# An adaptive-norm transformer kernel: start loads on two queues, block 0's key products on DVE, the last modulations on DVE, and instruction lists placed anew

## The chip, the cores and the metric

The kernel runs on one core of one Trainium2 chip. The metric is device time in microseconds (us), the median of three runs. Engines are called as in the profile: PE (matrix engine), DVE (vector), ACT (scalar activations), POOL (GpSimd), and SP, which here only issues DMAs. ACT can issue DMAs too.

## What is computed

Two layers over x of 8 batches, 256 tokens and 128 features, all float32. Each layer normalises, scales and shifts the tokens with per-batch values (the modulation) made from a conditioning vector.

```python
# layer 0
h  = layernorm(x)*(1+ca) + sa                 # per batch
q,k,v = silu(conv4(silu(h @ W.T)));  q,k l2-normalised;  a,b = sigmoid(h @ Wa.T), sigmoid(h @ Wb.T)
for t in range(256):                          # per batch and head (16 heads of 8)
    S = a*S - a*b*outer(S@k, k) + b*outer(v, k);   o[t] = q @ S
x = x + ga*(o @ Wo.T + bo)
h2 = modulate(layernorm(x));  x = x + gb*(h2 + moe(h2))   # router, 8 experts 128->512->128, the two highest
# layer 1
x = x + ga1*(ssd(modulate(layernorm(x))) @ Wout.T)        # decaying sums along the tokens
x = x + gb1*ffn(modulate(layernorm(x)))                   # butterfly-parametrised 128->512->128, gelu
```

The gates are kept away from zero before use (a sign times at least 0.25), and the 18 butterfly stages of the last feed-forward are folded into two weight matrices on PE while the kernel runs.

## The kernel before

Features (or 16 heads times 8) lie on the 128 partitions, tokens in the free dimension. The 256 tokens are cut into five **windows** of 32, 32, 64, 64 and 64 tokens (`TWS`), each for all 8 batches; a **block** is 32 tokens (8 blocks: 0, 1, then two for each of windows 2 to 4), a **chunk** is 4 tokens (8 to a block). The recurrence over tokens is solved chunk by chunk on DVE: `chunk_seed` (L2254), `chunk_delta` (L2259), `chunk_outer` (L2273) and `chunk_scan` (L2282), four instructions for each of 64 chunks. They need two things that DMAs replicate over the partitions for a whole block, the normalised keys (`spread_keys`, L600, 8 DMAs into `krep`) and the solved keys (`spread_solved`, L614, 8 DMAs, and one at L616, into `wrep`). The solved keys come from a small triangular solve on DVE for each window: products of key pairs (`key_pairs`, L3275, on POOL) are summed over heads on PE (`key_products`, L758), `couple` (L2218) multiplies them by decays, and three pairs of `solve_product` (L2233) and `solve_rest` (L2242) update `XX`, whose first value POOL's `value` and `signed_key` (L3255, L3285) make.

Before that, each window passes layer norm (`center` L690 and `variance` L702 on PE, `ln_square` and `ln_scale` L1470 to L1482 on ACT, `ln` L2140 on DVE), `modulate` (L2155 and L2157 on DVE for the first two windows and the first experts' input, which are the list `WIDE`, else L1495 on ACT, one instruction per batch), five projections on PE (`project`), their activations on ACT (`projected`, L1521), a convolution of four taps (`first_tap` L1553 on ACT, `tap` L2206 on DVE), l2 norms (`square_sums` on PE, `norms` and `inverse_norms` L1577 to L1589 on ACT), and on POOL `key` (L3238), `query` (L3246), `scaled_key` (L3263), and the recurrence's helpers `decays` (L3296) and `read_state` (L3309). Behind a window's recurrence come the output projection (`attn_out`), the router, and the experts: `first` (L859) and `second` (L874) on PE with `hidden` (L1649) on ACT and `mix` (L2296) on DVE. Units 4 and 5 are the two halves of the batches of the last window; the last ssd and feed-forward are done in two halves too (numbered 3 and 4).

Nothing is scheduled by a compiler. Each engine has a hand-written list of calls (PE's begins at L943, ACT's at L1712, DVE's at L2543, POOL's at L3362, SP's at L627), it works through it in order, and every dependence is a semaphore wait inside the helper. So a waiting call holds up all calls behind it in its own list. A DMA is issued at its place in the list of the engine that issues it: SP's `loads` (L562), then the copies; ACT issues the first constant matrix (`load_center`) and the experts' weights (`load_weights`, L1460 and L1461, 2 MB each). `fold_up(i)` and `fold_down(i)` on PE (L782 to L801) with `folded` on ACT (L1595, L1597) fold the butterflies; `fold_load` on SP (L590) brings later stages' matrices into a ring of 8. `fill` (L941) is a matmul whose result nobody reads.

```python
            def key_pairs(n, g):          # POOL
                pool.wait_ge(s_kb_done, n + 1)
            def solve_product(n, j):      # DVE
                if j == 0:
                    dve.wait_ge(s_xk_init, n + 1)
            def chunk_seed(w, i):         # DVE, first chunk that reads wrep
                    dve.wait_ge(s_wrep_in[h % 2], 16 * DH * (h // 2 + 1))
```

## Time and profile before

| | |
|---|---|
| median of 3 runs | 488.26 us (487.59 to 488.83) |
| the profiled execution's own time | 488.68 us |
| its span in the profile | 486.1 us |
| PE, DVE, ACT, POOL busy | 426.6, 343.3, 363.9, 165.6 us |
| mean granted TensorE clock | 0.979 |
| last scan of the recurrence starts | 323.7 us |
| last output DMA lands | 486.1 us |

The span runs from the first to the last event in the trace; 2.6 us of the profiled execution's time lie outside it. All places below are us from the span's start. A row of a timeline merges neighbouring instructions of one line: start, length of the group, engine, line, what it writes and reads, count, and in brackets how long the engine idled before it and what ended that. A busy engine in a row of windows is counted with its small pipeline gaps closed.

### The profile page before, as it was taken

Reading aid. Unit: us, or ns where it says so; the run is one execution under the profiler, and the core shown is the slowest. Engines: PE = TensorE matmul, PEld = TensorE weight load, DVE = VectorE, ACT = ScalarE, POOL = GpSimd, SP = SyncE. Lnnn points to the kernel's source line nnn. Section 1 sums busy time; section 2 is a strip of 40 time slices with the busy share of each in tenths; the row PEclk is TensorE's granted clock in tenths of the full one; section 3 lists DMA queues with packets and bytes.
Section 4 is the critical chain, followed back from the end, with each engine's and each line's share of the span. In section 5 each row is a group of like instructions: output and inputs, shape, how many; then the busy total and the mean of one; then the engine's idle time right before and its main releaser. Section 6 shows DMA issues by size and latency. Waiting matters only on the chain. (4 is left out here: it accounts for less than half of the span.)

```text
span 486.1 us, 7168 instructions
## 1 busy us (share of the span) xinstructions
PE 426.6 (88%) x2168; PEld 312.2 (64%) x2168; DVE 343.3 (71%) x876; ACT 363.9 (75%) x643; POOL 165.6 (34%) x236
## 2 busy tenths in 40 slices
PE   3498797869998699999999999999999878999666
PEld 2395674547776576757676656776676646798434
DVE  1545988877899984999999899998434681212751
ACT  4849688876985669889669794849988888646544
POOL 1060860684165963365940173161200001000010
PEclk9859999889999999999999999999999999999999
DMA  7999635012830228300204801000001000000000
GB/s 194 315 365 252 221 87 122 2 50 66 224 79 0 55 50 216 99 0 13 76 1 114 213 6 23 1 1 0 2 0 24 0 1 1 23 1 1 0 0 22
DMA packets 34484, 35.46 MB, mean 73 GB/s; under 512 B 12808, under 2 KB 30608, under 8 KB 34192
## 3 DMA queue, kind: packets, MB, share of 16 engines
q1 hardware_dynamic: 34016, 30.77, 23.9%
q10 hardware_dynamic: 432, 4.26, 2.3%
q8 instruction: 17, 0.28, 0.2%
q14 instruction: 19, 0.16, 0.1%
HBM read 13.78 MB, written 1.05 MB: 31 GB/s over the span
## 5 line engine op out<-in xcount | busy, mean ns | idle before, releaser
L874 PEld LDWEIGHTS psS<-we2s,hid 128*128 128x128 f32 x1024 | 130.5, 193 | 33.2 <-issue 29.5
L859 PE MATMUL psF<-h,we1s 128*128 128x256 f32 (+1 forms) x384 | 135.7, 461 | 9.0 <-ACT hid L1649 8.3
L874 PE MATMUL psS<-we2s,hid 128*128 128x128 f32 x1024 | 131.8, 277 | 5.5 <-DVE acc L2296 5.5
L1649 ACT ACTIVATE hid<-psF,col 128x256 f32<-128x256 f32 (+1 forms) x192 | 99.2, 542 | 48.4 <-PE psF L859 42.9
L859 PEld LDWEIGHTS psF<-h,we1s 128*128 128x128 f32 x384 | 65.6, 192 | 43.9 <-issue 21.6
L3309 POOL TENSOR_TENSOR QS<-H,qn 128x256 f32<-128x256 f32 x64 | 52.5, 834 | 96.8 <-DVE H L2282 74.7
L2296 DVE SCALAR_TENSOR_TENSOR acc<-psS,gate,acc 128x128 f32<-128x128 f32 x128 | 40.6, 342 | 44.4 <-PE psS L874 44.0
L2282 DVE TENSOR_TENSOR_SCAN H<-A,psT 128x320 f32<-128x320 f32 x64 | 52.1, 814 | 1.2
L2254 DVE TENSOR_TENSOR psT<-wrep,H 128x360 f32<-128x360 f32 x63 | 42.9, 681 | 10.4 <-DMA wrep<-XX 8.6
L1449 ACT ACT_TABLE_LOAD x37 | 47.5, 1283 | 1.8 <-PEq L3614 1.2
L3360 POOL TENSOR_TENSOR x<-x,gdb 128x512 f32<-128x512 f32 (+1 forms) x5 | 4.4, 870 | 130.0 <-PE psM L690 129.0
L1447 ACT ACT_TABLE_LOAD x29 | 37.2, 1283 | 0.8 <-issue 0.3
L3296 POOL COPY A<-ag 128x256 f32<-128x256 f32 x64 | 30.4, 493 | 13.9 <-DVE H L2282 13.9
L2206 DVE SCALAR_TENSOR_TENSOR zb<-p,col,zb 128x512 f32<-128x512 f32 (+1 forms) x45 | 27.3, 646 | 7.2 <-ACT zb L1553 7.1
L2259 DVE TENSOR_REDUCE psT<-psT 128x32 f32<-128x288 f32 x63 | 29.1, 462 | 1.5
L815 PE MATMUL psB<-QS,worep 128*128 128x256 f32 x128 | 29.1, 381 | 0.0
L2273 DVE TENSOR_TENSOR psT<-krep,psT 128x256 f32<-128x256 f32 x63 | 26.8, 426 | 1.9
L690 PE MATMUL psM<-x,C 128*128 128x512 f32 (+3 forms) x36 | 17.8, 578 | 11.2 <-DMA x<-xT_dram 7.3
L815 PEld LDWEIGHTS psB<-QS,worep 128*128 128x128 f32 x128 | 24.1, 190 | 5.0 <-issue 1.7
L702 PE MATMUL psB<-sq,C 128*128 128x512 f32 (+3 forms) x36 | 18.0, 585 | 1.8 <-ACT sq L1470 1.8
L1495 ACT ACTIVATE hS<-hS,mod 128x64 f32<-128x64 f32 x48 | 16.5, 432 | 0.6 <-DVE hS L2140 0.6
L2539 DVE SCALAR_TENSOR_TENSOR x<-psM,mod,x 128x64 f32<-128x64 f32 x28 | 5.7, 276 | 15.7 <-PE psM L934 15.7
(264 smaller groups left out, 656.3 us busy)
## 6 DMA issues: line engine op xcount, KB each, us to landing
wrep<-XX SPq DMA_DIRECT2D x72, 160.0 KB, 3.4
krep<-kn SPq DMA_DIRECT2D x64, 128.0 KB, 2.5
hid<-fold_mats_dram SPq DMA_DIRECT2D x22, 256.0 KB, 4.4
we1s<-we_dram ACTq DMA_DIRECT2D x1, 2048.0 KB, 7.9
we2s<-we_dram ACTq DMA_DIRECT2D x1, 2048.0 KB, 13.7
outT_dram<-x SPq DMA_DIRECT2D x3, 256.0 KB, 2.6
M<-mats_dram SPq DMA_DIRECT2D x1, 576.0 KB, 4.3
x<-xT_dram SPq DMA_DIRECT2D x2, 256.0 KB, 7.1
```

Of the source, the lines that this page charges most:

```text
L815: last = mm(psB[:, at:at + HC], worep[:, e, :], QS[:, e, :], start=(e == 0), stop=(e == DH - 1))
L859: mm(bank[name][:, 0:(b - a) * TWS[w]], we1s[:, e, k * P:(k + 1) * P], h2[w % 2][:, a * TWS[w]:b * TWS[w]], start=True, stop=True).then_in ...
L874: last = mm(bank[name][:, t * P:(t + 1) * P], hid[n % 2][:, k, t * P:(t + 1) * P], we2s[:, e, k, :], start=(k == 0), stop=(k == HT - 1))
L1447: nc.scalar.preload_act_table_set(LN_EXP)
L1449: nc.scalar.preload_act_table(kind)
L1649: nc.scalar.activation(hid[x_ % 2][:, k, 0:c], psF[n % 2][:, 0:c], ACT.Silu, bias=pc("be1", HT * e + k)).then_inc(s_hid_done, 1)
L2254: v_.tensor_tensor(T9[:, :, :, :], wv, prev.unsqueeze(3).broadcast_to([P, DH + 1, NB, C9]), ALU.mult).then_inc(s_prod_done, 1)
L2259: v_.tensor_reduce(U[:, :, :], T9[:, :, :, 1:].rearrange("p e b i -> p b i e"), AX.X, ALU.add).then_inc(s_u_delta, 1)
L2282: v_.tensor_tensor_scan(H[g % NH_][:, 0:DH, :, :].rearrange("p e b i -> p (e b i)"), A9[g % NA][:, :, :, :].rearrange("p e b i -> p (e b i)"),
L2296: v_.scalar_tensor_tensor(acc[w % 2][:, at, :], psS[n % 2][:, t * P:(t + 1) * P], gate[w % 2][:, at, e:e + 1], acc[w % 2][:, at, :], ALU.m ...
L3296: g_.tensor_copy(A9[g % NA][:, :, :, 1:], a).then_inc(s_a9_done, 1)
L3309: g_.tensor_tensor(o, H[g % NH_][:, 0:DH, :, 1:], q, ALU.mult).then_inc(s_qs_done, 1)
```

## The change

1. **Loads on two queues.** ACT, behind `load_center`, now issues the first three projection matrices (`M[:, 0:3]`); SP issues the other six behind the second window's x, and with them the rest of the modulation weights, which were ahead of it.
2. **Key products of window 0 on DVE.** `key(0)`, `scaled_key(0)`, `key_pairs(0, 0)` and `key_pairs(0, 1)` leave POOL's list and stand in DVE's (new helpers there). Windows 1 to 4 keep them on POOL.
3. **Last modulations on DVE.** `modulate` of ssd 3, ssd 4, ffn 3 and ffn 4 leaves ACT for DVE, as one `tensor_scalar` with two per-partition scalars for each batch (4 to a call). The modulation of window 1's layer norm no longer waits for the second modulation's values, which it does not read.
4. **Four of block 0's eight solved-key copies** are issued by ACT (`SPLIT = 4`, new `spread_solved` there), the other four and the ninth by SP.
5. **Lists placed anew** on all engines. In the start, PE's second modulation and `fold_up(0)` stand ahead of `square_sums(0, .)`, a `fill` ahead of them, `load_weights` stands behind `folded(12)` instead of behind the gates; in the middle `mix`, `first`, `second`, router and recurrence calls change places by a few positions; in the end `fill`s move.

```diff
@@ sync @@
+                    if n == 1:
+                        sp.dma_start(M[:, 3:, :], mats[:, 3:, :]).then_inc(s_rest_in, 16)
+                        sp.dma_start(wm[:, 0, 2 * P:], wmod[:, 0, 2 * P:]).then_inc(s_fold_in, 16)
+                        sp.dma_start(wm[:, 1, :], wmod[:, 1, :]).then_inc(s_fold_in, 16)
                     if n == 0:
...
-                        sp.dma_start(M[:, :, :], mats).then_inc(s_mat_in, 16)
-                        sp.dma_start(wm[:, 0, 2 * P:], wmod[:, 0, 2 * P:]).then_inc(s_fold_in, 16)
-                        sp.dma_start(wm[:, 1, :], wmod[:, 1, :]).then_inc(s_fold_in, 16)
...
-                for e in range(DH):
+                for e in range(0 if h else SPLIT, DH):
@@ tensor, project @@
+                if n == 0 and i == 3:
+                    pe.wait_ge(s_rest_in, 16)
@@ scalar @@
                 nc.scalar.dma_start(C[:, 0, :], consts[:, 0, :]).then_inc(s_center_in, 16)
+                nc.scalar.dma_start(M[:, 0:3, :], mats[:, 0:3, :]).then_inc(s_mat_in, 16)
...
+            def spread_solved():
+
+                act.wait_ge(s_x_sub, CH - 1)
+                for e in range(SPLIT):
+                    nc.scalar.dma_start(wrep[0][:, e, :], XX[e::DH, 1, 0:HC // CH, :].rearrange("p g i -> p (g i)").unsqueeze(1).broadcast_to(
+                        [HEADS, DH, H9])).then_inc(s_wrep_in[0], 16)
@@ scalar, list @@
+            folded(3)
+            spread_solved()
+            projected(1, 3)
@@ vector, modulate @@
+                if key not in WIDE:
+                    for i, b in enumerate(ln_batches(key)):
+                        last = v_.tensor_scalar(out[:, i, :], out[:, i, :], mod[:, 6 * l + c, b:b + 1], mod[:, 6 * l + s, b:b + 1],
+                                                ALU.mult, ALU.add)
+                    last.then_inc(s_ln_h, 1)
+                    return
@@ vector @@
+            def key_pairs(n, g):
...
+                dve.wait_ge(s_kb_done, n + 1)
+                dve.wait_ge(s_qn_done, n + 1)
...
+                    v_.tensor_tensor(KK[:, g, at:at + bc * i].rearrange("p (g i) -> p g i", i=i), b3[:, :, j + 1:],
+                                     k3[:, :, j:j + 1].broadcast_to([P, bc, i]), ALU.mult).then_inc(s_kk_done, 1)
@@ sync, list @@
             spread_keys(1)
             spread_solved(1)
+            spread_keys(3)
             spread_keys(2)
             spread_solved(2)
             spread_solved(3)
-            spread_keys(3)
             spread_keys(4)
```

POOL in window 0, before, from the first value of `XX` to its last update (`kn`, `bg` and `zb` are the keys, the scaled keys and the pair products):

```order
L3296 COPY A<-ag 128x64x4
L3255 TENSOR_TENSOR XX<-zb,bg 128x64x4
L3238 TENSOR_TENSOR kn<-zb,norm 128x256
L3263 TENSOR_TENSOR bg<-kn,bg 128x256
L3246 TENSOR_TENSOR qn<-zb,norm 128x256
L3275 TENSOR_TENSOR zb<-bg,kn 128x192
L3275 TENSOR_TENSOR zb<-bg,kn 128x64
L3296 COPY A<-ag 128x64x4
L3275 TENSOR_TENSOR zb<-bg,kn 128x128
L3296 COPY A<-ag 128x64x4 x2
L3285 TENSOR_TENSOR XX<-bg,XX 128x64x4
```

The same stretch of POOL with the change:

```order
L3273 TENSOR_TENSOR XX<-G,na 128x64x4
L3298 TENSOR_TENSOR XX<-zb,bg 128x64x4
L3289 TENSOR_TENSOR qn<-zb,norm 128x256
L3339 COPY A<-ag 128x64x4 x6
L3328 TENSOR_TENSOR XX<-bg,XX 128x64x4
L3352 TENSOR_TENSOR QS<-H,qn 128x64x4 x2
```

`kn`, `bg` and the three products of POOL's list are gone from it, and all six `A` copies now stand ahead of the `XX<-bg,XX` that the solve waits for. DVE with the change, from `kn` to the solve's first steps:

```order
L2211 TENSOR_TENSOR kn<-zb,norm 128x256
L2219 TENSOR_TENSOR bg<-kn,bg 128x256
L2231 TENSOR_TENSOR zb<-bg,kn 128x192
L2231 TENSOR_TENSOR zb<-bg,kn 128x64
L2231 TENSOR_TENSOR zb<-bg,kn 128x128
L2254 TENSOR_TENSOR G<-psS,G 128x64x3
L2254 TENSOR_TENSOR G<-psS,G 128x64
L2254 TENSOR_TENSOR G<-psS,G 128x64x2
L2269 TENSOR_TENSOR norm<-G,XX 128x2x192
L2242 SCALAR_TENSOR_TENSOR zb<-p,col,zb 128x256
L2278 TENSOR_TENSOR XX<-XX,norm 128x2x64x3
L2269 TENSOR_TENSOR norm<-G,XX 128x2x128
```

These five key steps are new there; `zb<-p,col` (a tap of window 1) stands inside the solve.

ACT with the change, from `folded(0)` to its DMAs of the solved keys:

```order
L1603 ACTIVATE ssdb<-psM 128x516
L1450 ACT_TABLE_LOAD
L1527 ACTIVATE p<-psS,col 128x8x32 x2
L1601 ACTIVATE wc<-psF 128x512
L1527 ACTIVATE p<-psF,col 128x8x32
L1603 ACTIVATE ssdb<-psM 128x516
L1559 ACTIVATE zb<-p,col 128x256
L1479 ACTIVATE sq<-psM 128x512
L1559 ACTIVATE zb<-p,col 128x256 x2
L1448 ACT_TABLE_LOAD
L1489 ACTIVATE sq<-psB,eps 128x512
L1491 ACTIVATE sq<-sq 128x512
L1601 ACTIVATE wc<-psF 128x512
L1469 DMA wrep<-XX 128x1x320 x4
```

The four `wrep` copies stand behind window 1's first activations and the layer norm of window 2; before, ACT had no DMA here.

SP around block 2, before (a digit is the buffer, so `krep0` and `wrep0` are block 2's):

```order
L600 DMA krep1<-kn 128x1x256 x8
L614 DMA wrep1<-XX 128x1x320 x8
L616 DMA wrep1<-XX 128x320
L600 DMA krep0<-kn 128x1x256 x8
L614 DMA wrep0<-XX 128x1x320 x8
L616 DMA wrep0<-XX 128x320
L614 DMA wrep1<-XX 128x1x320 x8
L616 DMA wrep1<-XX 128x320
L600 DMA krep1<-kn 128x1x256 x8
```

and with the change:

```order
L602 DMA krep1<-kn 128x1x256 x8
L616 DMA wrep1<-XX 128x1x320 x8
L618 DMA wrep1<-XX 128x320
L602 DMA krep1<-kn 128x1x256 x8
L602 DMA krep0<-kn 128x1x256 x8
L616 DMA wrep0<-XX 128x1x320 x8
L618 DMA wrep0<-XX 128x320
L616 DMA wrep1<-XX 128x1x320 x8
L618 DMA wrep1<-XX 128x320
```

Block 3's keys (`krep1`, which wait until block 1's last `chunk_outer` has read the buffer) are now ahead of block 2's keys and solved keys; the same swap is made for blocks 5 and 7.

## Rows read from the trace of the kernel before

**Rows 1.** The page's parts 1 and 2: busy us of each engine, granted clock by slice.

```profile
PE 426.6 (88%) x2168; PEld 312.2 (64%) x2168; DVE 343.3 (71%) x876; ACT 363.9 (75%) x643; POOL 165.6 (34%) x236
PEclk9859999889999999999999999999999999999999
```

**Rows 2.** Windows: start:end, length, then busy us (x instructions) of PE, PEld, DVE, ACT, POOL, clock, DMA share, GB/s.

```profile
60.00:200.00 140.00, 121.94 (x623) 91.36 (x623) 117.88 (x252) 109.90 (x209) 77.23 (x109) 0.98 0.36 91
200.00:350.00 150.00, 149.08 (x747) 101.98 (x746) 136.45 (x332) 118.95 (x183) 63.44 (x80) 1.00 0.15 37
444.00:486.00 42.00, 27.54 (x118) 18.37 (x116) 20.01 (x67) 21.90 (x53) 1.22 (x2) 1.00 0.03 7
```

**Rows 3.** Timeline of PE and ACT, the first window's start.

```profile
10.88 1.22 PE L690 MATMUL psM<-x,C 128*128 128x256 f32 x2 [2.65 <-DMA x<-xT_dram]
...
13.07 0.48 ACT L1521 ACTIVATE p<-psS,col 128x264 f32<-128x264 f32 x1 [3.16 <-issue]
```

**Rows 4.** Timeline of ACT, POOL and DVE, from the norms to the first step of solve 0.

```profile
27.00 0.63 ACT L1589 ACTIVATE norm<-norm 128x512 f32<-128x512 f32 x1
...
27.70 0.72 POOL L3238 TENSOR_TENSOR kn<-zb,norm 128x256 f32<-128x256 f32 x1 [0.78 <-ACT norm L1589]
...
32.97 0.70 POOL L3285 TENSOR_TENSOR XX<-bg,XX 128x256 f32<-128x256 f32 x1
...
34.59 0.69 DVE L2218 TENSOR_TENSOR G<-psS,G 128x192 f32<-128x192 f32 x3 [2.18 <-PE psS L758]
35.41 0.56 DVE L2233 TENSOR_TENSOR norm<-G,XX 128x384 f32<-128x384 f32 x1
```

**Rows 5.** Groups of ACT by form, 27.7 to 46: busy us, mean ns, idle before.

```profile
L1447 ACT ACT_TABLE_LOAD x1 | 1.3, 1283 | 0.0
L1597 ACT ACTIVATE ssdb<-psM 128x516 f32<-128x516 f32 x3 | 1.8, 590 | 2.9 <-PE psM L782 2.9
```

**Rows 6.** Timeline of DVE, one instruction's line alone and beside POOL.

```profile
9.11 0.43 DVE L2155 TENSOR_TENSOR hf<-hf,mod 128x264 f32<-128x264 f32 x1
...
31.13 0.63 DVE L2155 TENSOR_TENSOR hf<-hf,mod 128x256 f32<-128x256 f32 x1
```

**Rows 7.** SP's and DVE's timelines, the DMA view (KB each, us to landing), a window: solved keys of block 0.

```profile
28.45 7.60 SPq L600 DMA_DIRECT2D krep<-kn  x8
...
39.79 5.37 SPq L614 DMA_DIRECT2D wrep<-XX  x8
...
48.91 0.54 DVE L2254 TENSOR_TENSOR psT<-wrep,H 128x360 f32<-128x360 f32 x1 [4.45 <-DMA wrep<-XX]
...
wrep<-XX SPq DMA_DIRECT2D x72, 160.0 KB, 3.4
...
45.00:50.00 5.00, 4.63 (x35) 3.96 (x34) 1.02 (x3) 4.52 (x10) 1.30 (x4) 1.00 0.92 243
```

**Rows 8.** The DMA view and DVE's timeline: the experts' second weights, block 2's first seed.

```profile
we2s<-we_dram ACTq DMA_DIRECT2D x1, 2048.0 KB, 13.7
...
81.38 0.54 DVE L2254 TENSOR_TENSOR psT<-wrep,H 128x360 f32<-128x360 f32 x1 [0.20 <-issue]
```

**Rows 9.** Timelines of DVE and SP, block 1's last outer product to block 2's copies.

```profile
107.38 0.42 DVE L2273 TENSOR_TENSOR psT<-krep,psT 128x256 f32<-128x256 f32 x1
...
105.11 5.08 SPq L600 DMA_DIRECT2D krep<-kn  x8
118.57 5.34 SPq L614 DMA_DIRECT2D wrep<-XX  x8
```

**Rows 10.** Timelines of ACT, PE and DVE in the end.

```profile
471.64 1.42 ACT L1495 ACTIVATE krep<-krep,mod 128x64 f32<-128x64 f32 x4
...
473.88 1.28 ACT L1449 ACT_TABLE_LOAD   x1
...
478.35 1.89 PE L934 MATMUL psM<-krep,wc 128*128 128x256 f32 x8
...
449.15 0.86 DVE L2397 SCALAR_TENSOR_TENSOR x<-psS,mod,x 128x64 f32<-128x64 f32 x4 [0.53 <-PE psS L885]
```

More of the change, by code:

```diff
@@ L1325, in _ @@
                 first(4, 4, i)
-            fill(39)
+            second(4, 3, 0)
             first(4, 4, 3)
-            first(4, 5, 0)
-            second(4, 3, 0)
             second(4, 3, 1)
-            for i in range(1, 4):
+            for i in range(0, 4):
                 first(4, 5, i)
+            first(4, 6, 0)
             second(4, 4, 0)
             second(4, 4, 1)
-            first(4, 6, 0)
             ssd_out(2)
@@ L1380, in _ @@
             first(5, 4, 1)
-            center(("ssd", 3))
             second(5, 3, 0)
@@ L1789, in _ @@
             modulate(("front", 3))
-            for i in range(0, 3):
-                hidden(0, 3, i)
+            hidden(0, 3, 0)
+            hidden(0, 3, 1)
             projected(3, 0)
+            hidden(0, 3, 2)
             hidden(0, 3, 3)
@@ L2013, in _ @@
                 hidden(4, 3, i)
-            for i in range(0, 3):
-                hidden(4, 4, i)
+            hidden(4, 4, 0)
+            hidden(4, 4, 1)
+            ssd_factors(2)
             ssd_gate(2)
@@ L2055, in _ @@
             ln_scale(("ssd", 3))
-            modulate(("ssd", 3))
             ssd_steps(3)
@@ L2060, in _ @@
             ssd_in(3)
-            modulate(("ssd", 4))
             ssd_steps(4)
@@ L3485, in _ @@
-            for i in range(4, 8):
+            decays(3, 11)
+            for i in range(3, 6):
+                read_state(3, i)
+            decays(3, 12)
+            conv_taps()
+            read_state(3, 6)
+            decays(3, 13)
+            read_state(3, 7)
+            decays(3, 14)
+            value(4)
+            key(4)
+            read_state(3, 8)
+            attn_gate(4)
+            experts_gate(2)
+            read_state(3, 9)
+            decays(3, 15)
+            scaled_key(4)
```

1201 lines of the change are left out of this document (599 added, 602 removed).

## The prediction

> **What bounds the kernel now.** I read the page's busy line first: PE is the busiest engine and its granted clock is at the upper level (2.4 GHz) in nearly every slice, low only in single early ones [rows 1]. The windows then say where a change can pay. From 200 to 350 us PE is busy 149.08 of 150 us: there only less PE work, or work that comes earlier, shortens anything. From 60 to 200 it is busy 121.94 of 140, and in the last 42 us only 27.54, with DVE at 20.01 and ACT at 21.90 [rows 2]. In those last us no engine is full, so each step of the chain counts at its own length. The third view is the timeline ahead of the first seed of the recurrence: a chain of single instructions from the first activation through norms, keys and solve to DMAs. The recurrence, and with it most of what PE does later, hangs on it.
>
> **The loads.** The first `center` begins at 10.88, after 2.65 us of idle that a DMA of x ends; the first activation at 13.07 follows 3.16 us of ACT's idle [rows 3]. In the change x's second part no longer stands behind six projection matrices and most of the modulation weights, and `M[:, 0:3]` has SP's place to itself. The gain is at most the idle of 3.16 us, and it can be nothing if the bytes ahead of x were not what made it late; a loss here would need M's first part to come later than x, and it is the first thing on ACT's queue after one small constant. I take half, 1.5 us. The norms then end at 27.63 [rows 4] less 1.5, 26.1.
>
> **Key products on DVE.** Before: norms end 27.63, POOL's `kn` at 27.70 takes .72, and the last thing that the solve waits for, `XX<-bg,XX`, ends at 32.97 + .70; `couple` comes at 34.59 behind 2.18 us of waiting for PE, the solve at 35.41 [rows 4]. After: two 128x256 products at .63 each and 384 elements of pair products, some 1.05 us, end at 28.4 (.63 is the price of such an instruction beside POOL, .43 alone [rows 6]; by .43 it is 27.7). PE's key products then need banks that ACT's first activations of window 1 free. ACT passes one fold (.59), a table load (1.28) [rows 5] and two activations of .48 [rows 3], 2.8 us, so to 28.9, and `couple` (.69 [rows 4]) is done by about 30.2. POOL meanwhile has one product of .73, six copies of about .43 and the signed key at .70 (the prices of the products are from [rows 4], that of the copies is taken between .40 and .46), 6.0 less the first value of `XX` that it starts early, so about 30.3. All three meet at 30.4, where the solve starts, 5.0 us earlier, the loads' 1.5 included.
>
> Here a row speaks against the change: the same instruction on DVE took .43 us with POOL quiet and .63 with POOL at work [rows 6]. By these prices the moved work loses 46% to contention and is still shorter than POOL's chain. The Trainium skill ("SBUF — State Buffer", section "SBUF: two separate sides") calls this pair of ports an exclusive lock, held for a whole instruction of DVE with two SBUF inputs against one of POOL, and not a shared rate. By that rule POOL's nine instructions and DVE's five would alternate: 6.0 + 2.3 from 26.1, so the solve at 34.4, only 1.0 earlier.
>
> It needs no page to be a rival: the .20 of rows 6 could be a whole instruction's wait (.4 to .7) where both engines have denser work.
>
> **The solve** ran from 35.41 to SP's next issue at 39.79 [rows 4, 7], 4.35 us, with two taps of window 1 in it. In the change one of them (about .48) stands behind the solve, and the copies of constants too: 3.4 us, end 33.8, 6.0 earlier.
>
> **Spread of the solved keys.** SP's eight key copies took 7.60 us from 28.45 [rows 7]; they begin with `kn`'s end and, 1 to 2 us earlier, stay ahead of the solve's end as before. Nine issues of some .65 then end at 45.8, the first seed follows at 48.91 after 4.45 us of waiting for these DMAs, one copy taking 3.4 us to land; from 45 to 50 the DMA engines are busy to .92 at 243 GB/s [rows 7]. The split removes four issues from SP, 4 × .67 = 2.7 us by issue time. Against it: ACT reaches its four only behind some 13 activations of about .56 and two table loads of 1.28 [rows 3, 5], 9.8 us, with 1 us of waits for PE, so at 36.9, and issues till 39.6. Plus 3.4 that is 43.0. SP's five begin at 34.3 and end at 37.6. So the first seed comes at about 42.8, 6.1 earlier, and the split itself is worth nearly nothing. Were it free of ACT's list, it would be 40.8. The Trainium skill ("DMA: Bandwidth & Descriptors", section "Issuing engines are not separate DMA queues") has it that issuing on several engines saves only the issue time, all transfers running on the same 16 engines. With the share of .92 of rows 7 even the 2.7 us would be doubtful.
>
> ACT's own cost: 2.7 us of issue in front of `projected(1, 3)`, hidden as long as window 1 isn't the end of the chain (its first seed is some 20 us away); with the cover gone it is 2.7 us.
>
> **The middle.** The experts' second weights took 13.7 us to land [rows 8]. Issued behind `folded(12)`, at about 52, they are there by 66, and the first experts run at about 75: no cost, and the copies of block 0 no longer share the DMA engines with them. Window 1's chain is 5.5 to 6 us earlier too, since its inputs are, and block 2's first seed (81.38 [rows 8]) moves to about 75.5. From 200 us on PE has no idle in which an earlier arrival could be lost [rows 2], so the head's gain reaches the tail whole. I put the moves of `mix`, `router` and the rest at 0, between −3 (18 us of PE idle between 60 and 200 is there to be found [rows 2]) and +6 (the whole of the head's gain lost in it).
>
> **The tail.** `modulate` of ffn 3 took 1.42 us on ACT [rows 10], and four such instructions on DVE took .86 with a PSUM input [rows 10], so at most that: −.56. The table load at 473.88 stood behind ACT's work and now begins about .45 earlier, and the next modulation no longer splits ACT's gelu calls: the down projection that ran from 478.35 to 480.24 [rows 10] starts some 1.8 us earlier. I take −1.8 for the feed-forward, between −.5 (only the shorter modulation) and −3 (both modulations of 1.42 gone from ACT and the chain). In the ssd the same move gains .6 for half 4, but `ln` and `modulate` of half 3 now stand ahead of the residual that follows `experts` at 449.15 [rows 10] and delay it by .5 to .75: 0. Behind the waiting modulations DVE holds residuals that are not ready sooner, so the wait costs nobody.
>
> **The sum.** Head −6.1, middle 0, tail −1.8: −7.9 from the profiled execution's 488.68 gives 480.8. That execution is .42 above the median of the runs, so I forecast **480.5 us**.
>
> **Rivals.**
> - *The forecast's case*, 0.60: the head's shift passes through.
> - *Part of the head's gain is eaten*, 0.18: the port of rows 6 blocks for whole instructions (+4 by the working above), or ACT comes to its four copies 2 to 3 us late because of its two table loads and waits for PE. The seed then comes at 45 to 46. For it speaks that ACT's copies are the last of all steps in my sum; against it, that POOL's chain has been shortened by four instructions. Price 3 to 4 us: 484.
> - *The middle gains too*, 0.12: the moved calls fill some of PE's 18 idle us between 60 and 200, and the lower clock there goes. Some 3 us more: 477.5. Against: nothing in the rows shows that the places of these calls were what made PE wait.
> - *Slower than before*, 0.06: the order on SP. Before, SP issued block 2's keys from 105.11 for 5.08 us and its solved keys from 118.57 [rows 9]. Now block 3's keys stand ahead of both, and they wait for block 1's last outer product, which ended at 107.38 + .42 = 107.80 [rows 9]. Two sets of keys, 2 × 5.2, are 10.4 us of issue between 107.80 and 118.54, the end of the solve: room for 10.7. It just fits, if this distance is kept. But the last outer product comes earlier or later with the recurrence, the solve with PE's projections; each us by which the distance shrinks delays block 2's second set, hence all later chunks, by one. To lose more than the 7.9 gained and 1.5 besides, the distance must fall below about 1.3 us. At its worst the sum is 480.8 + 10.4 = 491. For: block 5's and 7's keys have the same swap. Against: the outer products move with the same head, so both ends shift together.
> - *The change doesn't do what it says*, 0.04: the second queue brings x no sooner (the bytes share the same engines) and the four copies wait behind ACT's list while the products on DVE wait for the banks that ACT frees. Then only the tail and part of the key chain are left: −3 to −4, 485.
>
> **Numbers.** The measurement can tell some 0.3%, 1.5 us, from no change. Forecast's case, eaten, middle and the failed second queue are all faster. A loss of up to 7 us in SP's order or the middle brings it to the same or near. Faster 0.87, the same 0.05, slower 0.08 (the 0.06 and other waits of the new lists). For the range: the forecast's own terms give −1.2 and +1.8 on the tail, ±1.5 on the loads, so 477.5 to 483.5; eaten and failed cases reach 485 to 486, the middle's case 476. Range 476 to 486; left out are the slower case, some of the eaten and the far end of the middle.
>
> **What would show it.** Right: first activation at about 11.5; solve starting at 30 to 31; the first seed near 43, waiting for the copies that ACT issued; block 2's first seed near 75.5; last scan of the recurrence near 318; first down projection 1.5 to 2 us nearer to the end; table load behind half 4's inverse root, with no L1495 between gelu calls. Wrong: the first activation still at 13 (loads), DVE's key products at .8 or more each (port), first seed beyond 45 (spread), a seed of block 2 or 3 waiting over 2 us for `wrep` (SP's order), a shift of the head of 6 us that is 3 at 200 us (middle), or experts' first matmul waiting for its weights.

## The result, and the profile after

The changed kernel takes **493.45 us** (median of 4 runs, 491.94 to 495.33); before, in the same comparison, 488.54. The ratio is 1.008, 95% interval 1.005 to 1.011: slower by 3.9 us (2.4 to 5.4). The forecast was 480.5 in a range of 476 to 486. All us of a difference below are a ratio times 489, with its interval.

The page's busy line and clock after, against [rows 1]. PE's busy time grew by 4.5 us and its mean clock fell from .979 to .969:

```profile
PE 431.1 (88%) x2164; PEld 313.1 (64%) x2164; DVE 351.3 (72%) x897; ACT 359.8 (73%) x627; POOL 166.9 (34%) x231
...
PEclk9878999979999899999999999999999999999899
```

The windows, with the columns of [rows 2]:

```profile
60.00:200.00 140.00, 120.11 (x594) 88.49 (x594) 114.55 (x244) 107.93 (x206) 74.81 (x100) 0.95 0.43 117
200.00:350.00 150.00, 147.31 (x739) 100.59 (x738) 140.07 (x333) 115.52 (x175) 65.68 (x84) 1.00 0.15 36
```

From 60 to 200 PE is busy 1.8 us less than before, at a granted clock of .95 instead of .98; from 200 to 350 again 1.8 us less: PE does less work in the same stretch. When the scans of the recurrence begin shows where the time went (us; in brackets the distance to before; block and chunk count from 0):

| scan of | before | changed | start and end only (r1) | middle only (r4) |
|---|---|---|---|---|
| block 0, chunk 1 | 50.59 | 48.69 (−1.9) | 48.39 (−2.2) | 50.28 (−.3) |
| block 2, chunk 0 | 129.20 | 127.94 (−1.3) | 127.54 (−1.7) | 128.84 (−.4) |
| block 3, chunk 6 | 169.92 | 170.57 (+.7) | 168.24 (−1.7) | 169.76 (−.2) |
| block 4, chunk 0 | 191.05 | 194.53 (+3.5) | 189.92 (−1.1) | 193.55 (+2.5) |
| block 6, chunk 0 | 272.09 | 280.92 (+8.8) | 270.84 (−1.3) | 280.54 (+8.5) |
| block 7, chunk 7 | 323.65 | 330.91 (+7.3) | 322.44 (−1.2) | 330.59 (+6.9) |

The changed kernel is still 1.0 us ahead when block 3 begins (151.36 for 152.39) and loses in two stretches, from there to block 4 and from block 4 to 6. From the last scan to the end of the span it takes 160.4 us where the kernel before took 162.5, so some 2 of the 7.3 us come back.

The start of the timeline, ACT and then PE, against [rows 3, 4]:

```profile
6.53 0.22 ACT L1459 ACTIVATE csil<-csil 128x16 f32<-128x16 f32 x1 [3.40 <-DMA col<-cols_dram]
...
11.21 0.39 ACT L1479 ACTIVATE sq<-psM 128x256 f32<-128x256 f32 x1 [1.84 <-PE psM L692]
11.61 1.28 ACT L1450 ACT_TABLE_LOAD   x1
12.90 0.85 ACT L1527 ACTIVATE p<-psS,col 128x264 f32<-128x264 f32 x2
...
25.81 0.84 ACT L1583 ACTIVATE norm<-psS,eps 128x256 f32<-128x256 f32 x2 [1.96 <-PE psS L751]
...
28.09 0.63 ACT L1595 ACTIVATE norm<-norm 128x512 f32<-128x512 f32 x1
...
9.98 1.19 PE L692 MATMUL psM<-x,C 128*128 128x256 f32 x2 [1.00 <-DVE hf L2143]
...
19.09 2.49 PE L720 MATMUL psM<-csil,wrep 128*128 128x8 f32 x20 [2.62 <-DVE hf L2143]
22.00 2.06 PE L786 MATMUL psM<-ssdb,hid 128*128 128x129 f32 x8 [0.42 <-DVE mod L2175]
23.86 1.91 PE L751 MATMUL psS<-norm,C 128*128 128x256 f32 x4
```

PE's `center` of window 1 no longer waits for x: it runs at 9.98 instead of 10.88. But ACT's first activation, which waits for the DMA of `col`, comes at 6.53 where it came at 5.61 (that DMA took 4.2 us to land, 3.3 before), and window 0's layer norm and modulation are 1.0 us later with it, done at 10.99. So the first projections begin at 11.14 instead of 11.89, .75 us earlier. ACT then squares window 1's layer norm at 11.21 ahead of its table load, and the first activation comes at 12.90 (13.07 before). Then PE's modulation and first fold (2.06 us from 22.00) stand in front of the square sums, and the norms' first activation waits 1.96 us for them. The last inverse norm ends at 28.72, 1.1 us later than before.

DVE's key products, the solve, the copies of the solved keys on SP and ACT, the first seed, and ACT's copies in the DMA view, against [rows 4, 7]:

```profile
28.83 0.98 DVE L2211 TENSOR_TENSOR kn<-zb,norm 128x256 f32<-128x256 f32 x1 [3.37 <-ACT norm L1595]
29.90 0.44 DVE L2219 TENSOR_TENSOR bg<-kn,bg 128x256 f32<-128x256 f32 x1
30.38 1.23 DVE L2231 TENSOR_TENSOR zb<-bg,kn 128x192 f32<-128x192 f32 x3
33.46 0.56 DVE L2269 TENSOR_TENSOR norm<-G,XX 128x384 f32<-128x384 f32 x1
...
37.79 3.36 SPq L616 DMA_DIRECT2D wrep<-XX  x4
...
39.72 2.25 ACTq L1469 DMA_DIRECT2D wrep<-XX  x3
...
47.15 0.54 DVE L2290 TENSOR_TENSOR psT<-wrep,H 128x360 f32<-128x360 f32 x1 [3.49 <-DMA wrep<-XX]
...
wrep<-XX ACTq DMA_DIRECT2D x4, 160.0 KB, 4.3
```

`kn` took .98 us, the other steps .44 and 1.23 for three. The solve starts at 33.46, 2.0 us earlier than before, and ends 2.2 earlier. SP issues four copies from 37.79 and ACT its last three from 39.72; the first seed stands at 47.15 instead of 48.91, after 3.49 us of waiting for these DMAs. From the first issue to the seed it is 9.4 us with two queues, 9.1 before with one, and ACT's copies took 4.3 us to land where SP's take 3.4.

PE's longest waits in the middle, and windows in which its clock was at the lower level (1.2 GHz) part of the time:

```profile
101.61 3.75 PE L878 MATMUL psS<-we2s,hid 128*128 128x128 f32 x16 [3.79 <-DVE acc L2332]
...
157.90 3.66 PE L751 MATMUL psM<-norm,C 128*128 128x512 f32 x4 [2.50 <-DVE x L2433]
...
168.07 3.01 PE L863 MATMUL psF<-h,we1s 128*128 128x256 f32 x6 [2.78 <-ACT hid L1655]
```

```profile
98.00:108.00 10.00, 6.39 (x24) 5.31 (x24) 6.57 (x14) 9.83 (x18) 6.92 (x7) 0.66 0.11 27
168.00:172.00 4.00, 3.93 (x14) 3.14 (x15) 3.90 (x8) 1.81 (x5) 3.92 (x5) 0.58 0.64 163
460.00:466.00 6.00, 4.54 (x12) 3.38 (x12) 5.71 (x18) 2.45 (x8) 0.00 (x0) 0.72 0.00 0
```

Before, past the start, PE's clock was at the lower level at 92 to 95 and 102 to 105 only. The changed kernel has a stretch of 7 us at 100 to 107 and others at 42 to 45, 157 to 161, 168 to 171 and 462 to 465, each at a wait of PE of 2.5 to 3.8 us.

SP's copies, and DVE's first seed and outer product for block 6. Changed:

```profile
246.73 5.84 SPq L602 DMA_DIRECT2D krep<-kn  x8
265.66 5.48 SPq L616 DMA_DIRECT2D wrep<-XX  x8
...
271.89 5.26 SPq L602 DMA_DIRECT2D krep<-kn  x8
...
273.77 1.63 DVE L2565 SCALAR_TENSOR_TENSOR x<-psM,mod,x 128x64 f32<-128x64 f32 x8 [1.22 <-PE psM L923]
275.32 0.53 DVE L2290 TENSOR_TENSOR psT<-wrep,H 128x360 f32<-128x360 f32 x1
...
280.46 0.43 DVE L2309 TENSOR_TENSOR psT<-krep,psT 128x256 f32<-128x256 f32 x1 [1.53 <-DMA krep<-kn]
```

and before:

```profile
228.98 5.04 SPq L600 DMA_DIRECT2D krep<-kn  x8
...
259.58 5.44 SPq L614 DMA_DIRECT2D wrep<-XX  x8
...
268.70 0.54 DVE L2254 TENSOR_TENSOR psT<-wrep,H 128x360 f32<-128x360 f32 x1 [1.28 <-DMA wrep<-XX]
...
271.44 0.42 DVE L2273 TENSOR_TENSOR psT<-krep,psT 128x256 f32<-128x256 f32 x1
```

Block 7's keys were issued at 246.73, and block 6's own keys only at 271.89, behind its solved keys; before, block 6's keys were issued at 228.98. So the first outer product of block 6 waited for `krep`, and it ran at 280.46 instead of 271.44. That wait is only part of these 9.0 us. The first seed of block 6, which reads no `krep`, is 6.6 us late already (275.32 for 268.70), and its solved keys are issued 6.1 us late. In front of it DVE now has an `ssd_residual` (L2565) that waited 1.22 us for PE and took 1.63; before, that call stood behind the seed. From the seed to the outer product it is 5.1 us instead of 2.7.

The end, against [rows 10]:

```profile
461.08 0.83 PE L904 MATMUL psS<-krep,M 128*128 128x256 f32 x2 [2.49 <-DVE krep L2159]
461.70 3.49 PE L915 MATMUL psB<-xi,taps 128*128 128x256 f32 x8
...
477.65 0.98 DVE L2159 TENSOR_SCALAR krep<-krep,mod 128x64 f32<-128x64 f32 x4
...
475.06 0.38 ACT L1479 ACTIVATE sq<-psM 128x256 f32<-128x256 f32 x1 [2.66 <-PE psM L692]
...
479.82 1.28 ACT L1450 ACT_TABLE_LOAD   x1
481.11 0.84 ACT L1715 ACTIVATE krep<-psM,ubias 128x256 f32<-128x256 f32 x2
...
483.53 1.89 PE L938 MATMUL psM<-krep,wc 128*128 128x256 f32 x8
```

The modulation takes .98 us on DVE for four (1.42 on ACT) and the table load is directly followed by the gelu calls. From ACT's square of the first feed-forward norm (475.06; 468.71 before) to the first down projection (483.53; 478.35 before [rows 10]) it is 8.5 us instead of 9.6. The eight matmuls of the first ssd convolution took 3.49 us at the lower clock; before they took 1.89.

### The profile page after: what moved, and what is told of

It is laid out like the page before. It is cut to its first block and busy times, and to the rows that moved or that the text cites. A ratio compares the mean times of both kernels' runs of the same rounds, so it can differ in the third digit from the quotient of the medians.

```text
span 491.3 us, 7161 instructions
## 1 busy us (share of the span) xinstructions
PE 431.1 (88%) x2164; PEld 313.1 (64%) x2164; DVE 351.3 (72%) x897; ACT 359.8 (73%) x627; POOL 166.9 (34%) x231
## 3 DMA queue, kind: packets, MB, share of 16 engines
HBM read 13.78 MB, written 1.05 MB: 30 GB/s over the span
## 5 line engine op out<-in xcount | busy, mean ns | idle before, releaser
L863 PE MATMUL psF<-h,we1s 128*128 128x256 f32 (+1 forms) x384 | 137.5, 464 | 8.9 <-ACT hid L1655 7.9
L878 PE MATMUL psS<-we2s,hid 128*128 128x128 f32 x1024 | 133.8, 278 | 8.5 <-DVE acc L2332 8.4
L1655 ACT ACTIVATE hid<-psF,col 128x256 f32<-128x256 f32 (+1 forms) x192 | 100.4, 543 | 54.1 <-PE psF L863 46.2
L3352 POOL TENSOR_TENSOR QS<-H,qn 128x256 f32<-128x256 f32 x64 | 55.0, 866 | 99.6 <-DVE H L2318 80.2
L3339 POOL COPY A<-ag 128x256 f32<-128x256 f32 x64 | 32.1, 525 | 0.0
```

Of the source, the lines that this page charges most:

```text
L863: mm(bank[name][:, 0:(b - a) * TWS[w]], we1s[:, e, k * P:(k + 1) * P], h2[w % 2][:, a * TWS[w]:b * TWS[w]], start=True, stop=True).then_in ...
L878: last = mm(bank[name][:, t * P:(t + 1) * P], hid[n % 2][:, k, t * P:(t + 1) * P], we2s[:, e, k, :], start=(k == 0), stop=(k == HT - 1))
L1655: nc.scalar.activation(hid[x_ % 2][:, k, 0:c], psF[n % 2][:, 0:c], ACT.Silu, bias=pc("be1", HT * e + k)).then_inc(s_hid_done, 1)
L3339: g_.tensor_copy(A9[g % NA][:, :, :, 1:], a).then_inc(s_a9_done, 1)
L3352: g_.tensor_tensor(o, H[g % NH_][:, 0:DH, :, 1:], q, ALU.mult).then_inc(s_qs_done, 1)
```

## The experiments

Sixteen kernels ran, each compared with the kernel before in the same set. "Middle" is all calls between about 60 us (PE behind `center(("front", 3))`, DVE from `chunk_seed(1, 0)`) and 444 us (PE from `second(5, 6, 0)`, DVE from `ln(("ssd", 3))`). A list put in another order holds the same calls, except that the changed order has no `fill(39)` in the middle.

How far single traces can be trusted shows in four kernels whose lists are those of before up to block 4, but for SP's in r6 (r3, r6, r8, r16): their scan of block 4 is −1.5, +.3, −.9 and −.1 us from that of before. So a distance to before of 1.5 us in one trace says little. From block 2 on such a distance changes by at most .6 us within one trace where the lists are the same.

| run | kernel | us, median | against before, us (interval) |
|---|---|---|---|
| | changed | 493.45 | +3.9 (2.4 to 5.4) |
| r1 | changed start and end | 487.70 | −1.6 (−2.8 to −.5) |
| r2 | changed start | 489.09 | −.1 (−1.0 to +.8) |
| r3 | changed end | 488.30 | −.6 (−1.9 to +.6) |
| r4 | changed middle | 494.84 | +5.0 (3.3 to 6.8) |
| r5 | changed, SP's order of before | 491.77 | +3.2 (2.2 to 4.3) |
| r6 | before, SP's changed order | 493.16 | +4.0 (2.6 to 5.4) |
| r7 | before, other lists 60 to 190 changed | 493.10 | +4.1 (2.6 to 5.5) |
| r8 | before, other lists 190 to 444 changed | 491.45 | +2.4 (1.5 to 3.3) |
| r9 | r1, start mended | 485.43 | −3.0 (−4.4 to −1.7) |
| r10 | r9 without the split | 485.53 | −3.2 (−4.4 to −2.1) |
| r11 | r7 with 2 unread matmuls | 490.79 | +2.1 (1.1 to 3.1) |
| r12 | r9 with 6 unread matmuls in the middle | 486.46 | −2.5 (−3.8 to −1.3) |
| r13 | r9 with 3 unread matmuls in the end | 485.64 | −3.3 (−4.5 to −2.1) |
| r14 | mended start, old end, modulations on DVE | 487.36 | −1.7 (−2.7 to −.6) |
| r15 | mended start only | 487.30 | −1.7 (−2.8 to −.5) |
| r16 | before, only block 7's keys moved on SP | 491.34 | +2.4 (1.5 to 3.3) |

### Which stretch (r1 to r4)

The theory was that the middle's order costs some 7 us; the rival, that the start's change harms the middle. r1 is the changed kernel with the middle's calls in the order of before:

```diff
             first(0, 0, 3)
-            logits(0)
             first(0, 1, 0)
-            second(0, 0, 0)
             first(0, 1, 1)
+            logits(0)
             first(0, 1, 2)
+            second(0, 0, 0)
...
```

> The changed kernel with its lists between about 60 and 444 us put back in the order of before; start (loads, key products, split copies, start of the lists) and end stay as changed. Theory O (the new order of the middle costs some 7 us, head gives about 1, tail about 2 to 3): about 485, 3 us under before. Rival P (the head's change itself harms the middle, by earlier but unevenly placed arrivals): 492 to 494, as the changed kernel.

Measured 1.6 us under before, at 487.7: the rival falls, and the theory's 485 was 2.7 too good. r2 takes the end back too (`modulate` of the four last norms on ACT again):

```diff
@@ vector @@
-            modulate(("ffn", 3))
@@ scalar @@
+            modulate(("ffn", 3))
...
```

> Only the start as changed, middle and end in the order of before, last modulations on ACT. Theory O: 487, 1 us under before, since the first seed of the recurrence came 1.8 us earlier in the changed kernel and PE is full from 200 us on. Rival P: 494 or more.

Measured −.1, and its profile's first chunk was 1.1 us later than before (51.66): the start is worth about nothing as it stands. The four traces with this start have the first seed at 47.15, 46.85, 50.12 and 48.56, the eight with the start of before between 48.43 and 49.62: on average .7 us earlier. r3 is before with the DVE helper and the end's lists of the change:

```diff
@@ vector @@
             ln(("ssd", 3))
+            modulate(("ssd", 3))
...
@@ tensor @@
-            fill(43)
...
```

> Only the end as changed: the four last modulations on DVE and the end's lists. Theory O and the tail's term of the prediction: 2 us under before, 486.5. Rival: the end as changed brings nothing because the stretch at the lower clock at 462 to 465 us of the changed kernel comes with it: 488 to 489.

Measured −.6 with an interval that holds both zero and the theory's −2. r4 is before with the changed order of the middle on all five engines:

```diff
             spread_solved(1)
+            spread_keys(3)
             spread_keys(2)
...
```

> The kernel before with nothing but the lists between about 60 and 444 us in the changed order. Theory O: 7 us slower than before, 495. Rival P: within 1.5 us of before.

Measured +5.0: the middle alone more than accounts for the loss, as theory O said; its size was 5 and not 7. The pieces that were changed outside the middle then take back 1 us.

### Which part of the middle (r5 to r8)

r5 and r6 undo and make SP's order alone:

```diff
-            spread_keys(3)
             spread_keys(2)
             spread_solved(2)
             spread_solved(3)
+            spread_keys(3)
...
-            spread_keys(7)
             spread_solved(6)
-            spread_keys(6)
...
```

> The changed kernel with nothing but SP's later copies put back in the order of before (block 2's keys and solved keys ahead of block 3's keys, and so for 5 and 7). Theory S (window 4's recurrence starts 8 us late because its first keys are issued behind block 7's keys and block 6's solved keys, and the end follows it): the first outer product of block 6 back to within 2 us of before, and the time at 487, 6 us under the changed kernel. Rival L (the lists of PE, DVE, ACT and POOL between 60 and 444 us cost the 5 us, PE being full while window 4 waits): 492 to 494, although block 6 starts earlier.

> The kernel before with nothing but SP's later copies in the changed order. Theory S: block 6's first outer product 8 us later than before and the time 5 us over before, 494. Rival L: block 6 late all the same, but the time within 1.5 us of before, since PE has experts' work to fill the wait.

r6 is 4.0 slower: SP's order does cost by itself, and PE's full stretch doesn't hide it. Its scans are within .7 us of before up to block 5 (191.31 for 191.05 at block 4) and 2.9 late at block 6. DVE waits there for `krep`, and PE then for the `mix` behind it on DVE:

```profile
274.36 0.43 DVE L2276 TENSOR_TENSOR psT<-krep,psT 128x256 f32<-128x256 f32 x1 [2.16 <-DMA krep<-kn]
...
283.50 1.73 PE L877 MATMUL psS<-we2s,hid 128*128 128x128 f32 x8 [2.26 <-DVE acc L2299]
```

But r5, where SP's order is put back in the changed kernel, is only .7 under the changed kernel, well inside the intervals, and its block 6 is still 7.3 us late (279.40). So theory S is right about a cost and wrong about it being the cause: in the changed kernel the other lists make block 6 late too, as its seed did above (275.42 in r5, 275.32 in the changed kernel). r7 and r8 take these lists alone, in two stretches:

```diff
@@ tensor, r7 @@
             attn_out(2)
-            square_sums(3, 0)
+            first(1, 3, 2)
             variance(("front", 4))
-            first(1, 3, 2)
+            square_sums(3, 0)
             square_sums(3, 1)
-            first(1, 3, 3)
             second(1, 2, 0)
             second(1, 2, 1)
+            first(1, 3, 3)
...
```

> The kernel before with PE's, ACT's, DVE's and POOL's lists between 60 and about 190 us in the changed order, SP as before. Theory S: within 1.5 us of before. Rival L: 2 to 4 us over before, since the changed kernel was 4 us behind at the first scan of window 3 (194.5 for 191.1).

> The kernel before with these lists between about 190 and 444 us in the changed order, SP as before. Theory S: within 1.5 us of before. Rival L: 1 to 3 us over before.

Rival L holds for both: +4.1 and +2.4. In r7 the distance to before is .7 at 170 us and 2.7 at the first scan of block 4, and stays at 3.2 to the last scan; window 3's solve begins at 177.22 and its solved keys are issued at 183.05, 180.09 before. In r8 it is −.9 at block 4, 4.1 at block 6 and 2.8 at the last scan. The three parts sum to 10.5 us and the whole middle costs 5.0. The traces show part of the overlap: from block 4 to block 6 r8 loses 5.0 and r6 2.7, but r4, which has both, 6.0; and from the last scan to the end r4 takes 161.6 us; r6, r7, r8 and before take 162.1 to 162.5. What the rest is was not followed.

### The clock (r11, r12)

r11 is r7 with two matmuls that nobody reads in PE's wait ahead of `second(1, 2, 0)`:

```diff
+            def fill_b():
+                free("B")
+                mm(psB[:, 0:4 * P], cst("ident"), C[:, :, :].rearrange("p a n -> p (a n)"), start=True, stop=True)
...
             square_sums(3, 1)
+            fill_b()
+            fill_b()
             second(1, 2, 0)
```

> The kernel of the seventh run (before, with the lists of 60 to 190 us in the changed order) plus two matmuls that nobody reads on the bank of the layer norm's variance, ahead of second(1, 2, 0), where PE idled 2.12 us and its granted clock then fell to 0.5 for 5 us. Theory C (the idle lets the clock fall, and this is most of the loss): no fall at 162 to 168, the shift of 3.2 us shrinks below 1, time 490 against the seventh run's 493.1. Rival W (the waits of the new order cost it, clock or no clock): 493.

The window 160 to 170 of r7, and then of r11:

```profile
160.00:170.00 10.00, 7.53 (x25) 5.54 (x26) 9.62 (x22) 7.39 (x10) 8.46 (x13) 0.66 0.10 24
```

```profile
160.00:170.00 10.00, 7.60 (x35) 5.37 (x34) 9.59 (x22) 7.93 (x11) 8.46 (x11) 0.86 0.23 57
```

The granted clock rose from .66 to .86; a lower stretch remains at 167 to 171. The runs put r11 at 2.1 us over before and r7 at 4.1, but the two intervals meet, and the profiles don't give the difference to the fill. r11's scans are 1.6 us ahead of r7's at the start of block 2 (128.06 for 129.68) and of block 3 (150.78 for 152.42), before anything differs in the lists; behind the fill they are 1.2 ahead at block 4 and 1.4 at the last scan. From block 3 to block 4 r7 loses 2.6 us and r11 3.0. So the higher clock gained nothing that these traces show, and rival W is left: the new order's waits cost the time, clock or no clock. r12 puts six into the mended kernel:

```diff
+            fill_b()
+            fill_b()
+            fill_b()
             second(0, 2, 0)
...
+            fill_b()
             square_sums(3, 1)
...
+            fill_b()
+            fill_b()
             second(1, 2, 0)
```

> The mended kernel of this set with six such unread matmuls: three ahead of second(0, 2, 0), where PE idled 3.74 us and the clock fell for 7 us, one ahead of square_sums(3, 1) and two ahead of second(1, 2, 0). Theory C: no lower clock between 98 and 108 and between 160 and 168, 5 us under the same kernel without them, 480. Rival W: the same time as without them, within 1 us.

The window 98 to 108 without them (r9) and with them (r12):

```profile
98.00:108.00 10.00, 7.87 (x30) 5.87 (x31) 6.83 (x16) 8.71 (x18) 9.06 (x11) 0.83 0.39 100
```

```profile
98.00:108.00 10.00, 7.06 (x32) 4.40 (x31) 6.86 (x16) 8.70 (x18) 9.37 (x13) 1.00 0.39 99
```

The clock is whole, and the time is the same within the intervals: 3.5 us ahead of before at block 4 instead of 3.4. So the lower clock there cost nothing that was on the chain, and theory C, with its 480, falls. The Trainium skill ("TensorE: Matmul & The Clock Gate", section "Part 1: The HAM clock gate") has PE fall to 1.2 GHz when it idles; the rows agree that a wait comes with each lower stretch named here (the shortest, .91 us, ahead of 447 in r9), and add that neither of the two filled here had a price that can be seen.

### The start (r9, r10, r15)

r9 is r1 with two calls moved:

```diff
@@ tensor @@
             modulation()
-            fold_up(0)
             square_sums(0, 0)
             square_sums(0, 1)
+            fold_up(0)
@@ scalar @@
-            ln_square(("front", 1))
             projected(0, 0)
             projected(0, 1)
+            ln_square(("front", 1))
```

> The first run's kernel (changed start and end, middle in the order of before) with two calls moved: PE's square sums of window 0 ahead of the first fold instead of behind it, and ACT's square of window 1's layer norm behind the first two activations, as before, instead of ahead of them and of their table load. Theory H (the new order of the start gave back what the loads and the key products gained): first activation at about 12.0 instead of 12.9, last inverse norm ended at 25.7 instead of 28.3 to 28.7, first seed at 44 instead of 47, time 3 us under the first run's 487.7, 484.7. Rival D (the spread of the solved keys over the DMA engines sets the first seed): norms 2.5 us earlier but the seed within 1 us of 47, time 487.

```profile
12.48 0.48 ACT L1547 ACTIVATE p<-psS,col 128x264 f32<-128x264 f32 x1 [1.77 <-issue]
...
23.89 0.84 ACT L1603 ACTIVATE norm<-psS,eps 128x256 f32<-128x256 f32 x2
...
26.18 0.63 ACT L1615 ACTIVATE norm<-norm 128x512 f32<-128x512 f32 x1
...
45.26 0.54 DVE L2354 TENSOR_TENSOR psT<-wrep,H 128x360 f32<-128x360 f32 x1 [4.12 <-DMA wrep<-XX]
```

The first activation comes at 12.48, the norms start at 23.89 without waiting, the last ends at 26.81 and the first seed is at 45.26, 3.7 us earlier than before, though later than the 44 of theory H. Rival D falls: against the changed kernel the norms' end and the seed both come 1.9 us earlier. The distance to before is 3.4 at block 2, 3.4 at block 6 and 3.4 at the last scan: what the start gains passes through the middle whole when the middle is in the order of before. How much it gains is less sure. Six traces have this start (r9, r10, r12 to r15), and they are ahead of before at block 4 by 3.4, 2.9, 3.5, 1.3, .8 and 3.0 us, 2.5 on average; the start alone, r15, is 1.7 faster in time. The time of r9 is 3.0 under before; it is the fastest of the kernels here, with r10, r12 and r13, which cannot be told from it.

r10 has SP issue all nine copies. The kernel that ran also had the two moved calls, which its expectation does not say, so it is to be read against r9:

```diff
-SPLIT = 4
+SPLIT = 0
...
             folded(3)
-            spread_solved()
             projected(1, 3)
```

> As the first run's kernel, with all nine copies of block 0's solved keys issued by SP and none by ACT. The prediction's term (the split is worth nearly nothing): first seed within 1 us of 46.5 to 47.2, time 487 to 488.5. Rival: issue time counts, and the seed comes 2.7 us later at 49.5, time 490.

First seed at 45.79 against 45.26, time within .2 us of r9: the split is worth nothing that can be measured. r15 leaves the end as it was:

```diff
@@ vector @@
-            modulate(("ssd", 3))
@@ scalar @@
+            modulate(("ssd", 3))
...
```

> The start as changed with the two calls moved, middle and end of before, modulations on ACT. The start's shift of 3.4 us passes through PE's full stretch whole: 485.5 to 486. Rival: the end as changed carried part of the ninth run's gain, and this is at 487.

487.3, 1.7 under before: the rival's figure, though its interval reaches to −2.8. So the end's change may carry 1.3 us of r9's 3.0, as between r2 and r1 (1.5); each of the two is inside the intervals. The profiles don't show this gain: from the last scan to the end the kernels with the changed end and the old middle take 161.7 to 163.1 us (r1, r3, r9, r10, r12, r13), before and r2 162.5 and r15 163.0.

### The end (r13, r14)

```diff
@@ r13, tensor @@
+            fill(61)
             ssd_steps(3)
...
+            fill(59)
+            fill(51)
             ssd_steps(4)
```

> The mended kernel of the ninth run with three more unread matmuls in the end: one ahead of ssd_steps(3) and two ahead of ssd_steps(4), where PE idled .91 and 2.49 us and its granted clock stood at 0.5 from 447 to 458. Theory C (the lower clock there costs the end part of its gain): no lower clock from 446 to 458, the 8 matmuls of the first ssd convolution take 1.9 instead of 3.6 us, and the time is 2 us under the ninth run's 485.4, 483.5. Rival: within 1 us of it, as the six fills of the middle were.

The first ssd convolution in r9, then in r13:

```profile
453.34 3.62 PE L918 MATMUL psB<-xi,taps 128*128 128x256 f32 x8
```

```profile
454.45 1.89 PE L918 MATMUL psB<-xi,taps 128*128 128x256 f32 x8
```

The eight matmuls take 1.89 us again, but the clock fell later (460 to 466) and the time is that of r9: no gain. r14 keeps the end's lists of before and puts each modulation on DVE behind its `ln`:

```diff
@@ vector @@
             ln(("ffn", 3))
+            modulate(("ffn", 3))
             ln(("ffn", 4))
+            modulate(("ffn", 4))
@@ scalar @@
-            modulate(("ffn", 3))
-            modulate(("ffn", 4))
```

> Mended start, middle and end in the order of before, the four last modulations on DVE directly behind their normalisation. If the modulations are the gain and the end's new order costs: 2 us under the run with the old end (r15), 484. If the new order of the end is part of the gain: 485 to 486.

The same as r15 (487.36 and 487.30), so neither the 484 nor the 485 to 486 came: the move of the modulations to DVE gives nothing without the end's new order.

### Which swap on SP (r16)

```diff
             spread_keys(5)
-            spread_keys(6)
+            spread_keys(7)
             spread_solved(6)
+            spread_keys(6)
             spread_solved(7)
-            spread_keys(7)
```

> The kernel before with only the keys of block 7 moved ahead of block 6's solved keys and keys on SP; the swaps of blocks 3 and 5 are not made. If the last swap is what costs on SP: the first scan of block 6 2.9 us late, 4 us over before, 493, as the sixth run. If it is the prediction's swap of block 3: the same time as before.

```profile
273.96 0.43 DVE L2276 TENSOR_TENSOR psT<-krep,psT 128x256 f32<-128x256 f32 x1 [2.60 <-DMA krep<-kn]
...
283.11 1.13 PE L877 MATMUL psS<-we2s,hid 128*128 128x128 f32 x8 [2.71 <-DVE acc L2299]
```

2.4 us slower, not 4; block 6 2.5 late, with DVE's wait for `krep` (2.60) and PE's for `mix` (2.71) as in r6. So the last swap is what costs on SP, and block 3's costs nothing that shows in r6 (its scan of block 3 is .1 late); r6's 1.6 more are within the intervals, and its profile alone had a stretch at the lower clock behind the same wait (284 to 287).

## Why the prediction was wrong, point by point

- **Two steps failed.** The forecast was 7.9 us faster, measured was 3.9 slower. Of these 12 us the start's term is 6.0 (forecast −6.1, r2 −.1), the middle's 5.0 (forecast 0, r4 +5.0) and the end's about 1 (forecast −1.8, r3 −.6). The middle's term made it a loss; without it the kernel is 1.6 faster (r1), still far from 7.9.
- **The middle.** The prediction put the moves of the middle at 0, between −3 and +6, and reasoned that from 200 us on "PE has no idle in which an earlier arrival could be lost". That holds for a shift of all work (r9: 3.4 us from block 2 to the last scan). It does not hold for a changed order: r4 measured +5.0 for it. PE's list waits for `mix` on DVE and DVE's for the recurrence, so a late block stops a full engine. The +6 stood among the bounds of the sum, as a loss of the start's gain; as a loss of the moved calls themselves it got no rival of its own, .02 of "other waits" and no place in the range.
- **SP's order, the rival on the other side.** The mechanism was right (keys issued ahead of what is needed sooner) and its place wrong. Block 2 lost nothing: its keys and block 3's were issued from 105.41 to 115.91, and its solved keys at 117.21. The third swap, that of block 7's keys, was mentioned as "the same swap" and not looked at. There SP had been idle from 252.6, and block 6's keys came 25 us after block 7's. Its price by r16 is 2.4 us alone; taken out of the changed kernel it gives back .7 (r5). The forecast gave this side .06.
- **The loads.** Taken at 1.5 us, measured .2 (first activation 12.90). Of ACT's idle of 3.16 PE's wait of 2.65 for x was the cause, and it did go; but the loads of the very start landed later, which left .75 us, and ACT's list had a square and a table load moved in front. With ACT's old order it is .6 (12.48 in r9). That the second queue could make the first loads later stood nowhere in the sum.
- **The norms.** Said to end at 26.1, ended at 28.72. The row of PE's order was in the change's description (modulation and first fold ahead of the square sums), and it was costed nowhere: the fold took 2.06 us at the lower clock. Mended, they end at 26.81 (26.7 to 27.9 in the six traces).
- **Key products on DVE.** Said to let the solve start 4.3 us behind the norms' end; it started 4.7 behind. DVE's steps took .98, .44 and 1.23, priced at .63, .63 and 1.05. The rival of whole instructions that block each other asked for 8.3 us behind the norms' end. That took POOL's work as 6.0 us, while the prices given for it add to 4.0 (4.7 with the first value of `XX`), and it ran 4.1; with these the rival asks for 6.3 to 7.0, and it falls even so; the Trainium skill's rule ("SBUF — State Buffer", section "SBUF: two separate sides") shows here at most in `kn`, .55 us over the uncontended .43, which began just behind POOL's product `qn`; `bg` took .44 with POOL's copies beside it. The solve ran 4.1 us instead of 3.4, as a tap that waited .76 us for ACT stood in it.
- **The split.** Said to be worth nearly nothing, and so measured (r10); the Trainium skill's rule ("DMA: Bandwidth & Descriptors", section "Issuing engines are not separate DMA queues") agrees. ACT's copies were said to be issued by 39.6 and were by 42.0. From first issue to first seed it is 9.3 to 11.7 us in the nine traces with two queues and 9.1 to 10.5 in the nine with one.
- **Head in sum.** Forecast −6.1; −1.9 at the second scan, −.1 us in time (r2). Mended, −3.4 in r9's trace, −2.5 on average of six, −1.7 in time (r15). So half of the term or more was never there.
- **The end.** −1.8 forecast, −.5 to −3 as bounds; measured −.6 (r3), −1.5 (r2 to r1), −1.3 (r15 to r9), none of them clear of the intervals, and not seen in the traces. The modulation on DVE was said to be .86 at most, and took .98.
- **A misread row.** The first seed at 81.38 [rows 8] is block 1's, not block 2's, which came at 127.59. In the changed kernel block 1's came at 81.02 and not at 75.5.
- **What would show it.** Of its signs of being wrong, the first activation at 13 (12.90), the first seed beyond 45 (47.15) and a shift lost by 200 us (+3.5) came true, and the one written for SP named block 2 or 3 instead of 6. Of the signs of being right, the table load with no modulation between the gelu calls came true.

Left open: which single moves in the lists of r7 and r8 cost (the `ssd_residual` ahead of block 6's seed stands in r4, r5, r8 and the changed kernel, and was not undone alone), and where in the end its gain is, if there is one. The end's lower clock was filled without gain, and its cause was not followed further.

## What to carry to other kernels

Where an order is written out by hand for five engines, the order itself is a tuned part: it is to be costed stretch by stretch for each engine, or undone alone in an experiment, before any gain at the start is counted. A full engine passes a shift through whole, but it waits as soon as a late block holds a partner that it reads. And the worth of a part is to be read from several runs: traces of one and the same start differed by 2.7 us at block 4. For copies queued on one issuer, the first use of each copy should be set beside its place in the queue for every block, not for the first one of a kind.

## What was not expected of the hardware

- The lower clock comes and goes between executions of one list. r9 and r13 have the same lists up to the end, and the clock was at .5 from 83 to 86 and from 100 to 103 in r9's profile, from 40 to 46 and from 102 to 105 in r13's. r1 and before have the same middle, and r1's profile had it at .5 from 161 to 167, before's not at all; its scans at block 4 were still only .6 us later relative to block 3.
- One 128x256 product on DVE took .98 us beside POOL (`kn`, in all ten traces that have it), the next .44 or .45, where [rows 6] had .63 and .43.
- With ACT's first part of M issued at 1.20 us, `col` (31.5 KB on SP's queue, issued at 2.32) took 4.2 us to land; without it 3.3. SP's queue behind `col` is another too, so the two aren't told apart.
- Four 128x64 `tensor_scalar` with two scalars took .98 us on DVE, four `scalar_tensor_tensor` of that size .86.
